# Last tile of the recurrence: mix and scale moved ahead of the shared gates, logits and routing two half steps earlier

## The reference

```python
def step(W, kv):                       # 32 steps of 16 tokens, 16 heads of 32
    kc, vc = kv
    z = einsum('bhsd,bhde->bhse', kc, W)
    grad = einsum('bhsd,bhse->bhde', kc, (z - vc) * inv_n)
    return (W - LR * grad, z)
...
x = layernorm(x + layernorm_affine(zs) @ Wo.T)
...
probs = softmax(x @ w_gate)            # 8 experts, the best 2 per token
routed = sum of the chosen experts' silu(g) * u @ w_down, weighted
shared = silu_and_mul(x @ w_sh_gate_up) @ w_sh_down
out = layernorm(x + routed + shared)
```

## Time and profile before

| what | value |
|---|---|
| runs, us | 692.97, 689.24, 691.87 (median 691.87) |
| the profiled execution | 693.32 us, its span 691.5 us |
| mean granted TensorE clock of the span | 0.989 |
| busy, us of the span | PE 666.4, DVE 428.3, ACT 298.9, POOL 295.3 |
| DMA, mean | 134 GB/s |
| chain that ended last | PE 54%, DVE 18%, POOL 9%, issue 7%, ACT 5%, DMA 4% |

### The profile page before, as it was taken

One profiled execution on the slowest core, in us unless ns is written; L12 is line 12 of the kernel. 1 busy time (PEld: TensorE's weight loads), 2 busy tenths in 40 slices (PEclk: granted clock), 3 DMA queues, 4 the chain that ended last, 5 costly groups with the idle time before them and its releaser, 6 DMA issues.

```text
span 691.5 us, 16510 instructions
## 1 busy us (share of the span) xinstructions
PE 666.4 (96%) x6880; PEld 534.6 (77%) x6880; DVE 428.3 (62%) x750; ACT 298.9 (43%) x520; POOL 295.3 (43%) x308
## 2 busy tenths in 40 slices
PE   9889999998999999999999999999999999999994
PEld 7656777776777777787887888888887888888883
DVE  5787766776845345488866544554456267676655
ACT  5534434542654432441123456655677442142232
POOL 0745666766736531011005335343552244726232
PEclk9989999999999999999999999999999999999998
DMA  8210152232351532100063578667657765414212
GB/s 283 83 65 20 50 174 80 85 109 63 112 171 50 171 98 91 45 1 0 1 244 114 177 265 299 199 245 256 207 161 259 261 185 175 123 61 127 72 76 91
DMA packets 65710, 92.47 MB, mean 134 GB/s; under 512 B 16672, under 2 KB 31776, under 8 KB 65632
## 3 DMA queue, kind: packets, MB, share of 16 engines
q1 hardware_dynamic: 59952, 72.76, 31.2%
q0 software_dynamic: 5680, 18.62, 9.5%
HBM read 67.56 MB, written 23.79 MB: 132 GB/s over the span
## 4 chain that ended last, share of the span: by engine, by line
PE 54%; DVE 18%; POOL 9%; issue 7%; ACT 5%; DMA 4%; SPq 0%; DVEq 0%; POOLq 0%; ACTq 0%
PE bank L1305 7%; PE zbank L1268 6%; PE wbank L1268 6%; PE zbank L1181 5%; PE bank L1073 4%; PE bank L1128 4%; PE wbank L1181 4%; PE bank L1194 3%; DVE x L1460 3%; POOL xg L1830 2%; DMA xg<-yd,SI 2%; PE zbank L1281 2%; DVE x L1508 2%; PE bank L1181 2%; PE zbank L1091 2%
## 5 line engine op out<-in xcount | busy, mean ns | idle before, releaser
L1792 POOL TENSOR_TENSOR xl<-RAW,xh 128x1024 fp32r<-128x1024 f32 x23 | 55.5, 2412 | 122.7 <-ACT xh L1659 122.6
L1675 ACT ACTIVATE ah<-sg 128x512 fp32r<-128x512 f32 x48 | 30.3, 632 | 158.4 <-DVE sg L1450 158.4
L1805 POOL DMA_INDIRECT xg<-x1d,idxu x39 | 42.0, 1078 | 69.8 <-DVE idxu L892 41.3
L1440 DVE TENSOR_TENSOR GL<-RAW,GH 128x1024 fp32r<-128x1024 f32 x42 | 50.3, 1223 | 11.0 <-ACT GH L1654 9.6
L1452 DVE TENSOR_TENSOR al<-sg,ah 128x512 fp32r<-128x512 f32 x48 | 34.1, 711 | 33.5 <-ACT ah L1675 33.5
L1194 PE MATMUL bank<-xh,ah 128*128 128x512 f32 x128 | 51.2, 400 | 1.7 <-DVE x L1460 1.0
L1830 POOL DMA_INDIRECT xg<-yd,SI x32 | 35.4, 1106 | 38.6 <-DVE x L1508 24.1
L1073 PE MATMUL bank<-xh,GH 128*128 128x512 f32 x112 | 49.0, 438 | 2.4 <-DVE shuf L1346 2.4
L1194 PE MATMUL bank<-xh,al 128*128 128x512 f32 x128 | 49.9, 390 | 0.0
L1194 PE MATMUL bank<-xl,ah 128*128 128x512 f32 x128 | 49.9, 390 | 0.0
L1450 DVE TENSOR_TENSOR sg<-sg,zbank 128x512 f32<-128x512 f32 x22 | 15.1, 685 | 53.1 <-PE zbank L1268 36.4
(11 more groups left out here) (302 smaller groups left out, 1773.3 us busy)
## 6 DMA issues: line engine op xcount, KB each, us to landing
RAW<-in_wgu SPq DMA_DIRECT2D x13, 1024.0 KB, 6.5
yd<-RAW SPq DMA_DIRECT2D x39, 256.0 KB, 4.7
RAW<-in_wsgu SPq DMA_DIRECT2D x14, 512.0 KB, 5.1
RAW<-in_wd SPq DMA_DIRECT2D x13, 512.0 KB, 5.8
x<-in_xtok SPq DMA_DIRECT2D x16, 256.0 KB, 3.4
x1d<-x SPq DMA_DIRECT2D x16, 256.0 KB, 2.3
RAW<-in_wsd SPq DMA_DIRECT2D x8, 512.0 KB, 4.8
out_x<-x SPq DMA_DIRECT2D x16, 256.0 KB, 2.0
```

What stands on the lines that cost most here:

```text
L1440: e.tensor_tensor(GL[:, w % 2, k:k + 2, :], gate_raw(w, k), GH[:, w % 2, k:k + 2, :].bitcast(F32), ALU.subtract).then_inc(*mark("low", "g" ...
L1792: e.tensor_tensor(DL[:, w % 2, :, :], draw[:, raw_of(w), :, :], DH[:, w % 2, :, :].bitcast(F32), ALU.subtract).then_inc(*mark("low p", "d" ...
L1805: e.indirect_dma_start(place(s), None, x1d, bass.IndirectOffsetOnAxis(ap=idxu[:, LINES[s]:LINES[s] + 1], axis=0)).then_inc(*mark(f"dma xg{ ...
```

## The change

`LAST`, the last half step, is 69 instead of 71. For tile 15 the steps "mix" and "x1" are written at n = 67, right behind its output product, instead of at 68 and 69; its "x1 turn" at n = 68 instead of 70 and its logits at 69 instead of 71. Logit group 1 and its rows come at n = 66 and 67 instead of 69 and 70. The half step two before the last draws 1.4 of budget on top of `DRAIN` instead of 2.0. No instruction is added or taken away.

```diff
-LAST = 4 * NT - 4 + 11
+LAST = 4 * NT - 4 + 9
...
-        tiles = {d: (n - d) // 4 for d in range(3, 12) if (n - d) % 4 == 0 and 0 <= (n - d) // 4 < NT}
+        tiles = {d: (n - d) // 4 for d in range(3, 12) if (n - d) % 4 == 0 and 0 <= (n - d) // 4 < NT - (d > 7)}
+        if n >= 4 * NT + 4:
+
+            tiles.update({10: NT - 1} if n == LAST - 1 else {11: NT - 1})
...
             do("wo", tiles[7], left[7])
+            if tiles[7] == NT - 1:
+                do("mix", NT - 1)
+                left[7] = ("mix", NT - 1)
+                do("x1", NT - 1)
...
-        for q_, at in ((0, 49), (1, 69)):
+        for q_, at in ((0, 49), (1, 66)):
...
-        budget += 0 if n < 47 else SCAN[n % 4] if n < 64 else DRAIN + 2.0 * (n == LAST - 2)
+        budget += 0 if n < 47 else SCAN[n % 4] if n < 64 else DRAIN + 1.4 * (n == LAST - 2)
```

## The result

The changed kernel took **695.5 us** (median of 16 runs, 693.0 to 697.7), the kernel before 690.7 us (16 runs, 687.8 to 693.1). The ratio is 1.0068 with a 95% interval of 1.0051 to 1.0086: slower by 4.8 us between the medians, 3.5 to 5.9 us by the interval. The predicted time was 696.5 us, and the predicted difference 4.6 us.

The account below looks back on a forecast made before the run. TensorE's own queue was taken as the bound from 260 to 400 us. Stall 3.5 + clock 1.3 + 0 + 0 − 0.2 = +4.6 us on the median 691.87 gave 696.5 us, range 693.3 to 699.3.

Parts of the forecast that it names:

- The forecast's case: TensorE stalls at group 1's small transposes and its clock falls after: +4.6 us, 696.5 us; chance 0.60.
- Term 1, the stall: Group 1's transposes on TensorE wait for ScalarE's copy of tile 14's logits, held behind tile 15's scale: 3.5 us.
- Term 2, the clock: TensorE's granted clock falls to 0.50 after the stall, slowing its matmuls: +1.3 us, with 0 and 1.6 as ends.
- Terms 3 and 5, moves and waits removed: Tile 15's transposes and logits and group 1's product moved: 0; wait for the counts' copy at 316.1 us gone: −0.2.
- Term 4, VectorE's margin: With routing earlier among the gates, VectorE's selection for route 7's counts delays TensorE by 0, up to 1.3 us.
- The prediction's better case: Reduction runs beside GpSimd: selection at E + 20.5, TensorE at counts E + 21.6; E ends the first gate unit's last matmul.
- three of three: All three TensorE waits of about 2 us or more had the clock at 0.50 for over 3 us behind them.
- Stall alone, clock kept: Rival: stall at the transposes, but no clock fall or one wholly within the stall: 695.2 us, +0.48%; chance 0.17.
- Late VectorE: Rival: stall, clock, and a reduction blocked by GpSimd (1.3) or route 17 waiting (0.6): 697.8 to 698.4 us; chance 0.13.
- Not slower: Rival: no stall at the transposes, earlier routing closes waits at 316 and 379 us: 691.1 us; chance 0.06.
- the signs of being wrong: No wait at group 1's transposes, a clock staying at 1.00, or a loss of time behind 380 us.

Follow-up runs that it names:

- the fill of 14: Changed kernel plus 14 matmuls of 512 columns, results unused, on TensorE ahead of the four small transposes: 692.9 us, ratio 1.0027 to the kernel before.
- the rows one half step later: Changed kernel with group 1's logit rows at n = 68, behind the rest of the first gate: 688.9 us, ratio 0.997 to the kernel before.

## Why the prediction was right

The forecast's case came, by its mechanism and in its place. Its sum, 4.6 us, stands against 4.8 between the medians and 5.15 in the measured stretch. That it came so close is in part luck: the clock cost 1.5 us more than it was priced at, the stall 0.3 us less, and the moves and removed waits gave back 0.7 us more, which leaves 0.5 in the stretch. The predicted time, 696.5 us, lies 1.0 above the measured one because it starts from the median of three runs, 691.87, where 16 runs gave 690.7.

**Term 1, the stall: right.** Predicted 3.5 us, with 3.3 to 3.7 as ends. From the end of the logits' issue (270.91 + 0.80 = 271.71, the 0.80 us as before) to the transposes at 275.08 it is 3.37 us. The idle time that the view of waits lists is 3.21, and the wait's time alone costs 3.2 in the stretch, both a little under the lower end. The link that carried the estimate, mix to scale, was predicted as 3.04 us from tile 15's own steps before; it is 274.15 − 271.11 = 3.04. That a wait in the queue of the engine that bounds the kernel costs its full length is shown by the fill of 14 against the rows one half step later: 3.2 us of time kept ahead of the transposes make the stretch 3.2 us longer, at the full clock in both.

**Term 2, the clock: right in kind, mis-sized.** Predicted +1.3 us with 0 and 1.6 as ends; it is 2.8 (2.6 to 2.8 by the four profiles with a fall), outside the ends. The failed step is "a stretch of 3.3 us thus holds some 8 of them where 14 or 15 would fit": all three waits that I read had one such length behind them, and I took it for the length of the fall in general. Here it was 6.8 us, about double, in four of four profiles in which it fell. The remark that a longer wait would hide part of the slow stretch helped little: of the 6.8 us only 0.5 to 0.9 lay in the wait in the four profiles, since the clock fell near its end. The argument "three of three" was too strong as well: behind waits of the same kind other executions kept the clock, as the twelve profiles show. A sounder upper end would have been a fall of unknown length, not of the length seen.

**Terms 3 and 5, moves and waits removed: right in sign, mis-sized.** Everything but the stall is worth −0.87 us, where the prediction had −0.2. One failed step is to price a removed wait at the idle time that the view of waits shows. Before, 24 down products around the wait for the counts took from 312.91 to 318.97, 6.06 us; now they begin at 315.71 and take 5.44. Of these 0.62 us, 0.46 belong to a wait listed as 0.2: the gap between starts was 315.51 to 316.10, 0.59 instead of 0.23, and the first matmul behind it took 0.33. (0.09 more is the slow first matmul behind the counts, 312.91 to 313.23. It has not gone but stands in the next gate now, 310.15 to 310.47.) The counts themselves take 0.1 less: 312.21 to 312.91 before, 309.56 to 310.15 now. The remaining 0.3 I can trace to no one place. The wait of 0.56 us at the rows gate stayed (0.54), as predicted.

**Term 4, VectorE's margin: the number right by luck, its reason not put to the test.** I took 0 for a late selection. The prediction's better case said 1.1 us early (E + 20.5 against E + 21.6), and the trace shows 1.1 (308.66 against 309.79). But the reduction that GpSimd's operation was expected to fall upon ran from 304.75 to 305.96, and GpSimd began at 305.84. What it fell upon instead was L767, an operation with two inputs, which took 1.32 us; L760, the same operation before, took 0.28. So VectorE lost 1.0 us that the case had not counted, and won about as much that it had not counted either: its wait for the exponential on ScalarE, 1.72 us before (at 295.26), was 0.38 now (at 293.98). L767 ends just behind GpSimd's operation, at 308.39 against 308.25. This is once more the contention that L754 showed, and the Trainium skill's rule (SBUF — State Buffer, Who interferes with whom) agrees in that half: two SBUF inputs contend. L1467, which reads one of its inputs from PSUM, ran beside the same GpSimd operation in its normal 1.28 us for two. Whether a reduction is free of it stays open.

**The rivals.** *Stall alone, clock kept* is what the fill of 14 builds: +2.35 us in the stretch, against the +3.3 that I gave it. *Late VectorE* had no place: no wait at the counts. *Not slower* needed a chain shorter by 3.5 us; moving the copy or the rows did just that, and gave −0.66 and −0.87 us, close to the −0.8 that I had put down for it, though not by the gathers I named: the wait at the rows gate is 0.55 us in the best kernel too. That rival was refused for the right reason. Of the signs of being wrong none came: a loss of time behind 380 us, for which the prediction had no term, is not there (311.9 and 311.8 us).

## What to carry to other kernels

Before an operation is moved ahead in one engine's queue, look at the operations that it passes, and at what the bounding engine waits for among them. Here a 0.8 us scale with a 3 us chain before it passed a 0.15 us copy that TensorE needed next; either one of the two moves alone cost 0.0 or 0.5 us. When a wait on TensorE cannot be avoided, price it in two parts, its length and a slow clock behind it, and take the second as something that comes in full or not at all in an execution: here it was 2.6 to 2.8 us behind idle waits of 2.2 to 3.2 us in four of four profiles, and nothing behind 1.5 us in two of two. Idle work in place of the wait can save the second part only; the first comes back only when the awaited result comes sooner or the waiting work later. Compare such kernels over a stretch between two fixed instructions; it repeated within 0.2 us here, where the totals of two executions of one kernel differed by up to 5.6.

## What was not expected of the hardware

- Whether the clock falls behind a wait, and for how long, is no fixed property of the kernel. Behind waits of 2.2 to 3.2 us at this place the granted clock was 0.50 for 6.8 us in four of four profiles. Behind the wait for `shuf`, 2.4 us between the same matmuls in all twelve profiles, it was so for 3.4 us in five and not at all in seven. Every fall behind a wait in the twelve profiles, with TensorE at work again, lasted 3.4 or 6.8 us; what decides between them no run shows.
- A wait listed as 0.2 us cost about 0.5: the gap between two starts was 0.59 us instead of 0.23, and the next one 0.33.
- The changed kernel's totals spread over 4.6 us in 16 runs and one more gave 701.0, with the measured stretch unchanged. The 5.6 us between its two profiles are accounted for: 2.7 lie ahead of the measured stretch, where the second has two more slow stretches of 3.4 us (near 41 and 161 us); 1.6 in the wait near the end, 0.4 us in one and 2.0 in the other; and some 1.5 (an estimate) in the slow stretch behind that wait.
